# A graph kernel's projection with wo: the last 30 rows of wo in four groups of 32 array rows, results in the upper halves of four banks

## The reference, cut to what matters

```python
norm_x = t5_layer_norm(hidden_states, ln_weight)
y = jax.nn.elu(rgcn_conv(norm_x, edge_index, edge_type, W_rel, W_root, conv_bias))  # 1250 x 286
y = y @ wo_weight                                                                  # 286 x 1024
return hidden_states + y
...
x = _layernorm(x + _L0_gnn_ref(...), axis=-1)   # so x1 = layernorm(2x + elu(...) @ wo)
# second network: h = layernorm(x) * g + b; h = relu(h @ W1 + b1) @ W2 + b2; three graph layers; decoder
```

## Time and profile before

| | |
|---|---|
| median of 3 runs | 587.81 us (587.09 to 589.5) |
| profiled execution | 587.64 us |
| its span, first to last instruction | 585.8 us |
| mean granted TensorE clock | 0.992 |
| stage of the change (aggregation of ten tiles with projection) | about 167 to 273 us of the span |
| one steady tile of it | 10.3 us |

### The profile page before, as it was taken

The page is one execution under the profiler, slowest core; times in us unless marked ns, Lnnn a source line. Parts: engine busy times, 40 slices in busy tenths (PEclk is TensorE's granted clock), DMA queues, the critical chain, the costliest instruction groups (busy, mean ns, idle before and its releaser), DMA issues.

```text
span 585.8 us, 8370 instructions
## 1 busy us (share of the span) xinstructions
PE 570.0 (97%) x2584; PEld 395.6 (68%) x2584; DVE 379.7 (65%) x980; ACT 231.6 (40%) x477; POOL 100.7 (17%) x80
## 2 busy tenths in 40 slices
PE   7999999999999999999999999999999999999992
PEld 3556656665577676775898888877878867455541
DVE  7599888888847888888602330018748667755455
ACT  5444455533224546463421221013223134276555
POOL 3000000000000000003165512402202230132230
PEclk8999999999999999999999999999999999999997
DMA  9510011111031121128300000700100100021123
GB/s 270 145 35 10 27 36 35 35 35 35 0 92 37 35 72 37 38 76 237 129 27 0 0 0 1 223 4 1 38 0 0 36 1 0 2 70 49 58 70 105
DMA packets 20870, 30.73 MB, mean 52 GB/s; under 512 B 5428, under 2 KB 15254, under 8 KB 20838
## 3 DMA queue, kind: packets, MB, share of 16 engines
q1 hardware_dynamic: 20422, 29.66, 17.2%
q10 hardware_dynamic: 416, 0.67, 0.4%
HBM read 25.20 MB, written 5.12 MB: 52 GB/s over the span
## 4 chain that ended last, share of the span: by engine, by line
PE 94%; DMA 2%; DVE 2%; ACT 1%; POOL 0%; SPq 0%; issue 0%
PE banks L744 20%; PE banks L943 12%; PE banks L1029 12%; PE banks L863 12%; PE banks L730 5%; PE banks L833 5%; PE banks L965 4%; PE banks L955 4%; PE banks L892 4%; PE banks L894 4%; PE banks L873 3%; PE banks L1019 3%; PE banks L837 2%; PE banks L848 1%; PE banks L738 1%; DMA cb_b<-in_L_gnn_conv_bias 1%
## 5 line engine op out<-in xcount | busy, mean ns | idle before, releaser
L744 PE MATMUL banks<-w_all,xnT 128*125 128x429 f32 x320 | 130.4, 532 | 1.9 <-DMA w_all<-in_L_gnn_W_rel 1.9
L744 PEld LDWEIGHTS banks<-w_all,xnT 128*125 128x125 f32 x320 | 54.6, 190 | 32.1 <-issue 29.7
L1192 DVE TENSOR_TENSOR adj<-adj,banks 125x220 f32 x160 | 60.8, 380 | 19.5 <-PE banks L730 17.4
L863 PE MATMUL banks<-hT,w_s 128*128 128x250 f32 x320 | 68.7, 375 | 0.1
L863 PEld LDWEIGHTS banks<-hT,w_s 128*128 128x128 f32 x320 | 60.2, 189 | 8.8 <-issue 1.9
L892 PE MATMUL banks<-y_hi,adj 125*125 125x288 f32 x200 | 55.2, 304 | 0.2 <-issue 0.2
L894 PE MATMUL banks<-y_lo,adj 125*125 125x286 f32 x200 | 53.5, 294 | 0.0
L730 PEld LDWEIGHTS banks<-oh_code,oh_low 125*128 125x128 bf16 x320 | 31.0, 97 | 32.0 <-issue 27.9
L1174 DVE TENSOR_TENSOR oh_code<-iota_c,edge 125x880 bf16<-125x880 f16 x80 | 48.7, 609 | 0.0
L1336 DVE TENSOR_SCALAR hT<-banks,g_c,b_c 128x125 f32<-128x125 f32 x60 | 19.4, 400 | 45.1 <-PE banks L848 45.0
L943 PE MATMUL banks<-adj,h_hi 125*128 125x250 f32 (+1 forms) x180 | 48.2, 367 | 0.0
(11 more groups left out here) (206 smaller groups left out, 884.4 us busy)
## 6 DMA issues: line engine op xcount, KB each, us to landing
xt<-in_x SPq DMA_DIRECT2D x15, 448.0 KB
out_x<-ot SPq DMA_DIRECT2D x9, 448.0 KB
w_s<-in_L_gnn_W SPq DMA_DIRECT2D x5, 512.0 KB, 6.0
xn<-in_x SPq DMA_DIRECT2D x5, 448.0 KB
wd_s<-in_L_gnn_Wd SPq DMA_DIRECT2D x1, 2048.0 KB, 13.7
w_all<-in_L_gnn_W_rel SPq DMA_DIRECT2D x6, 286.0 KB, 6.8
wo_s<-in_L_gnn_wo_weight SPq DMA_DIRECT2D x1, 1024.0 KB, 6.5
w_all<-in_L_gnn_W_root SPq DMA_DIRECT2D x3, 286.0 KB, 6.4
```

The source lines that it names most:

```text
L744: ins = pe.matmul(pb[0:P, 2 + 2 * v + n, 0:FH], xnT[:, u], w_all[:, u, n * FH:(n + 1) * FH], start=(u == 0), stop=(u == KD - 1))
L863: ins = pe.matmul(pb[:, 4 + f % 2, 0:2 * P], w1_s[:, k, f * 128:(f + 1) * 128], hT[:, k], start=(k == 0), stop=(k == KD - 1))
L1192: dve.tensor_tensor(cols, cols, window(b, q), ALU.add).then_inc(done, 1)
```

## The change

It adds two constants, Q = 4 and QW = 256. The columns of wo are cut into four quarters. Each quarter has its own results bank, 4 + q, and there the upper half, columns 256 to 511. The last 30 rows are four logical matmuls on array rows 32q to 32q + 29. The transposes go to the lower halves of banks 4 and 5 (before: all in bank 4). Therefore `turn_elu(t)` gets a wait for `res_done`; the last tile's transposes go to banks 2 and 3 instead, and the second half of `turn_chunk(0)`, which writes those, gets a wait for `yT_copied`. Since bank 4 still holds results when the encoder begins, the first block of chunk 0 goes to bank 0, and chunk 0 is written out in front of the loop. `wo_mm` counts 4 per tile. SP loads the last rows of wo four times, a quarter each; VectorE writes the tails four times (120 elements of a 128-wide buffer) and reads the four half banks in the residual.

```diff
+Q, QW = 4, D // 4
...
-            ("ybuf", [P, 5, F], F32), ("yT", [128, 3, P], F32), ("tails", [P, 64], F32), ("mv", [P, T, 4], F32),
+            ("ybuf", [P, 5, F], F32), ("yT", [128, 3, P], F32), ("tails", [P, 32 * Q], F32), ("mv", [P, T, 4], F32),
...
-            for q in range(2):
-                sp.dma_start(wo_s[32 * q:32 * q + FB[2], 2, q * 512:(q + 1) * 512],
-                             wo[256:F, q * 512:(q + 1) * 512]).then_inc(wo_in, 16)
+            for q in range(Q):
+                sp.dma_start(wo_s[32 * q:32 * q + FB[2], 2, q * QW:(q + 1) * QW],
+                             wo[256:F, q * QW:(q + 1) * QW]).then_inc(wo_in, 16)
...
-            def turned(t):
+            def turned(t, b=4):
                 act.wait_ge(yT_ps, t + 1)
-                act.wait_ge(wo_mm, 1 + 2 * t)
-                act.copy(yT[:, 0:2].rearrange("p k n -> p (k n)"), pb[:, 4, 0:2 * P])
-                act.copy(yT[0:64, 2], pb[0:64, 4, 2 * P:3 * P]).then_inc(yT_copied, 1)
+                act.wait_ge(wo_mm, 1 + Q * t)
+                act.copy(yT[:, 0:2].rearrange("p k n -> p (k n)"), pb[:, b, 0:2 * P])
+                act.copy(yT[:, 2], pb[:, b + 1, 0:P]).then_inc(yT_copied, 1)
...
-            turned(T - 1)
+            turned(T - 1, 2)
...
-            def turn_elu(t):
+            def turn_elu(t, b=4):
 
                 pe.wait_ge(elu_done, t + 1)
+                if t > 0 and b == 4:
+                    pe.wait_ge(res_done, t)
                 for i in range(2):
-                    pe.transpose(pb[:, 4, i * P:(i + 1) * P], ybuf[:, 4, i * 128:(i + 1) * 128], ident[0:P, 0:P])
-                pe.transpose(pb[0:64, 4, 2 * P:3 * P], tails[:], ident[0:P, 0:P]).then_inc(yT_ps, 1)
+                    pe.transpose(pb[:, b, i * P:(i + 1) * P], ybuf[:, 4, i * 128:(i + 1) * 128], ident[0:P, 0:P])
+                pe.transpose(pb[:, b + 1, 0:P], tails[:], ident[0:P, 0:P]).then_inc(yT_ps, 1)
             def project(t):
...
-                for q in range(2):
+                for q in range(Q):
                     for i in range(2):
-                        pe.matmul(pb[0:P, 5 + q], yT[:, i], wo_s[:, i, q * 512:(q + 1) * 512],
+                        pe.matmul(pb[0:P, 4 + q, 512 - QW:512], yT[:, i], wo_s[:, i, q * QW:(q + 1) * QW],
                                   start=(i == 0), stop=False)
-                for q in range(2):
+                for q in range(Q):
                     rows = slice(32 * q, 32 * q + FB[2])
-                    ins = pe.matmul(pb[0:P, 5 + q], yT[rows, 2], wo_s[rows, 2, q * 512:(q + 1) * 512],
+                    ins = pe.matmul(pb[0:P, 4 + q, 512 - QW:512], yT[rows, 2], wo_s[rows, 2, q * QW:(q + 1) * QW],
                                     start=False, stop=True)
                     ins.then_inc(wo_mm, 1)
-            def turn_chunk(c):
+            def turn_chunk(c, shared=False):
                 for u in range(2):
+                    if shared and u == 1:
+                        pe.wait_ge(yT_copied, T)
...
-            turn_elu(T - 1)
-            turn_chunk(0)
+            turn_elu(T - 1, 2)
+            turn_chunk(0, True)
             project(T - 1)
 
-            with pe.Fori(0, T // 2 - 1) as c:
+            chunk_of_3(0, False, 0)
+            with pe.Fori(1, T // 2 - 1) as c:
                 chunk_of_3(c, False)
...
-                dve.scalar_tensor_tensor(tails[:].rearrange("p (q n) -> p q n", q=2)[:, :, 0:FB[2]], twice(exps), -1.0,
-                                         twice(above), ALU.add, ALU.add).then_inc(elu_done, 1)
+                dve.scalar_tensor_tensor(tails[:].rearrange("p (q n) -> p q n", q=Q)[:, :, 0:FB[2]], copies(exps), -1.0,
+                                         copies(above), ALU.add, ALU.add).then_inc(elu_done, 1)
...
-                dve.wait_ge(wo_mm, 1 + 2 * (t + 1))
+                dve.wait_ge(wo_mm, 1 + Q * (t + 1))
                 dve.wait_ge(x_in, 32 * (t + 1))
-                dve.scalar_tensor_tensor(x1(t), xt[:], 2.0, pb[0:P, 5:7].rearrange("p a b -> p (a b)"),
+                dve.scalar_tensor_tensor(x1(t).rearrange("p (q n) -> p q n", q=Q), xt[:].rearrange("p (q n) -> p q n", q=Q), 2.0, pb[0:P, 4:8, 512 - QW:512],
                                          ALU.mult, ALU.add).then_inc(res_done, 1)
```

More of the change, by code:

```diff
@@ L330, in _ @@
             sp.dma_start(wa_s[:], wa[0].rearrange("(k p) f -> p k f", p=128)).then_inc(wab_in, 16)
-            sp.wait_ge(wo_mm, 1 + 2 * T)
+            sp.wait_ge(wo_mm, 1 + Q * T)
             for a, d in ((bd2_b, bd2), (go_b, g_out), (bo_b, b_out)):
@@ L542, in weigh_first, with relus_of_3 @@
                 ins.then_inc(hT_lo, 1)
-            def relus_of_3(c, blocks):
+            def relus_of_3(c, blocks, b0=4):
                 for f in blocks:
@@ L548, in relus_of_3 @@
                     act.wait_ge(r1_mm, 1 + c * K1 + f + 1)
-                    act.activation(r1T[:, f], pb[:, 4 + f % 2, 0:2 * P],
+                    act.activation(r1T[:, f], pb[:, b0 if f == 0 else 4 + f % 2, 0:2 * P],
                                    ACT.Relu, bias=b1_c[:, f:f + 1]).then_inc(r1_done, 1)
@@ L568, in _ @@
             first_norm(T - 2)
-            relus_of_3(0, [0])
+            relus_of_3(0, [0], 0)
             first_sd(T - 1)
@@ L850, in turn_chunk, with chunk_of_3 @@
                         ins.then_inc(xhT_ps, 1)
-            def chunk_of_3(c, last):
+            def chunk_of_3(c, last, b0=4):
                 pe.wait_ge(hT_lo, 1 + c + 1)
@@ L862, in chunk_of_3 @@
                     for k in range(KD):
-                        ins = pe.matmul(pb[:, 4 + f % 2, 0:2 * P], w1_s[:, k, f * 128:(f + 1) * 128], hT[:, k],
+                        ins = pe.matmul(pb[:, b0 if f == 0 else 4 + f % 2, 0:2 * P], w1_s[:, k, f * 128:(f + 1) * 128], hT[:, k],
                                         start=(k == 0), stop=(k == KD - 1))
@@ L897, in relations @@
                     if t == 1:
-                        pe.wait_ge(wo_in, 48)
+                        pe.wait_ge(wo_in, 16 + 16 * Q)
                     if t > 0:
@@ L1258, in _, with copies @@
             sums, below, exps, above, elu = (ybuf[:, i] for i in range(5))
-            def twice(a):
-                return a[:, 256:F].rearrange("p (o n) -> p o n", o=1).broadcast_to([P, 2, FB[2]])
+            def copies(a):
+                return a[:, 256:F].rearrange("p (o n) -> p o n", o=1).broadcast_to([P, Q, FB[2]])
             def relations(t, b, adj):
```

## The result

The changed kernel took 585.36 us in the median of 8 runs (583.42 to 586.65), the kernel before 587.75 us in 8 runs beside it. The ratio is 0.9956, with a 95% interval of 0.9941 to 0.9972: 2.4 us faster between the medians, 0.44% by the ratio. In a second comparison it gave 0.9945 (0.9930 to 0.9960). The forecast was 584.2 us, in a range of 583.3 to 586.8. The profiled execution took 585.49 us with a span of 583.7.

A forecast was written before the change was run, and what follows sets the result against it. TensorE, busy for 97% of the span, was taken as the bound; nine tiles at 0.40 us give 3.6, less 0.11 for tile 0, 3.5 us off 587.64: 584.1, written as 584.2 us, range 583.3 to 586.8.

The forecast's parts named there:

- the line of a plain forecast: Whole time 584.9 us, about 0.5% (2.9 us) faster, distinguishable from no change; faster than that had chance 0.59.
- Four groups at once: Projection's last 30 rows: four row groups run together, block 0.63 us, 0.42 less; net 0.40 us less per tile.
- The rival of pairs: Projection's last 30 rows: only two row groups run at a time, block stays 1.05 us, whole time 587.9; chance 0.13.
- the one of groups in a row: Projection's last 30 rows: row groups run one by one, block 1.92 us, whole time 595.7; chance 0.04.
- A round costs more with four: Rival, projection's last 30 rows: each round 0.3 of a pass longer, 0.13 us per tile, whole time 585.4; chance 0.10.
- The added wait costs 0: Transposes waiting for the previous tile's residual: load 0.04 us late, up to 0.09 free, price 0 with 0.05 to spare.
- The rival of a pace set by VectorE: Residual or its signal reaches the transposes 0.25 us later: 1.4 us over seven tiles, whole time 585.6; chance 0.14.
- Eight tiles keep 0.40: Aggregation's loop, tiles 0 to 7, TensorE the bound: each keeps the 0.40 us gain, 8 x 0.40.
- Projection 8 is lost to xh: Before the encoder handover: TensorE comes 0.40 us earlier but waits 0.75 us for xh, not 0.35; nothing kept.
- Projection 9 keeps 0.40: Last projection, behind the xh wait: hT ready about 272.7, TensorE wants it at 273.03, so the 0.40 us is kept.
- Tile 0: First tile's tails on the chain: wider write 0.06 us, larger clear taken as 0.05, together +0.11 us once.
- wo's four small loads, ScalarE's copy, the new wait's cover: Side edits: SP's smaller transfers 0 (upper bound 0.8 us), 128-partition yT copy 0, last chunk turn's yT wait covered.

## Why the prediction was right, and where its sum was off

The direction and the range were right, and so was the mechanism of the gain; one term of the sum failed and two were mis-sized. Forecast gain 3.5 us, measured 2.4 (2.6 or 3.2 by the two comparisons' ratios); from the first transpose to the last matmul 397.13 and 397.18 us became 394.31 and 394.15, so 2.8 to 3.0, less 0.1 in tile 0. The 0.6 to 0.8 us that are missing there are in the terms below; the rest of the first comparison's distance is no larger than the scatter of the first stage. 585.36 us also lies on the far side of the 584.9 that was drawn as the line of a plain forecast, where the prediction had put its rivals (0.4% gain in the first comparison, 0.55% in the second).

- **Four groups at once**: right. Block 0.64 for 0.63, full-height part 3.46. Two groups alone give 1.06 and no gain. The rival of pairs and the one of groups in a row fall.
- **A round costs more with four**: falls too. Two rounds take 0.44 us with four groups for 0.43 of two passes, by the block of the kernel with two groups. The passes' records are 476 and 374 ns, apart by 0.10 as 689 and 587 were; nothing is added within a round. By an estimate from the Trainium skill's 3.07 times (TensorE: Matmul & The Clock Gate, Part 3) a round would have been 1.3 passes, 0.56 us for two; the trace doesn't agree, and what keeps the block of 0.64 us above half of before (1.05) is the 0.2 us for entering and leaving.
- **The added wait costs 0**: the step that failed. The sum had the residual seen 0.05 us after its end, a load 0.04 late, and 0.09 free. The end of the residual was forecast exactly (6.60). But the load starts 0.115 after it, because the late wait stands second behind another, so it is 0.10 late, of which some 0.07 are free. That leaves 0.03 to 0.04 in each of tiles 2 to 8, 0.18 and 0.26 in the loops of the two profiles. With one wait the forecast's reckoning comes true: 79.34 us. The rival of a pace set by VectorE had this path and put 0.25 us more on it, 1.4 us in all; it is right in kind, with less than a fifth of the price.
- **Eight tiles keep 0.40**: 82.48 - 79.34 = 3.14 without the wait's price, 2.96 and 2.88 with it; forecast 3.2 (8 x 0.40).
- **Projection 8 is lost to xh**: right (the load waits 0.6 us for xh, 0.75 was forecast, 0.35 before), and 0.12 more is lost, which the forecast set at nothing: it counted neither GpSimd beside the wider tails nor the second wait.
- **Projection 9 keeps 0.40**: mis-sized, 0.34 in the one profile and 0.08 in the other. I had checked hT and not what follows. Relu and norm of tile 9 on ScalarE, behind tile 9's x, came just in time for block 3 in the kernel before (the relu ended 0.18 us ahead of it), and TensorE's lead ran into them.
- **Tile 0**: clear and tails were set at 0.11; in the chain the clear's step is longer by 0.06 and the tails' by 0.06, 0.12 in all.
- **wo's four small loads, ScalarE's copy, the new wait's cover**: no wait names them; 0 each. The new wait for yT costs its 0.06 us only by standing in front of the late one.

## What to carry to other kernels

Short contractions that already run in two row groups can run in four: here the streaming time halved again, 0.86 to 0.43 us, and the fixed 0.2 us for entering and leaving stayed. Before a gain on the bounding engine is counted, look at each neighbour whose margin is smaller than that gain, and also at the stage after: here VectorE took back 0.03 us in each of seven tiles, GpSimd and a second wait 0.12 once, and a late x and ScalarE's order up to 0.3 once. In this kernel an added wait that came last cost less as the only one in front of its instruction; moving the work that it waits for forward in its engine's order did the same. Where runs scatter by more than the edit is worth, compare stages inside the traces, and look at the granted clock of each stage before a difference is put down to loads.

## What the runs showed of the hardware that was not expected

- A late wait that stands behind another one starts TensorE's load 0.115 us after the signalling instruction's end, a lone one 0.05 us after. It was so for VectorE's and for GpSimd's signal, and taking one wait away undid it in both places. Why, the trace doesn't show, and no run tries the two waits in the other order.
- A small VectorE instruction of 0.21 us in front of a large one delayed the large one's end by 0.08 us only.
- GpSimd's instruction grew by just as much (0.06 us) as VectorE's beside it, and shrank again with it.
- The same program ran its first products with w_all at 1.2 or at 2.4 GHz. In both profiles of the kernel before the first of them begins at 8.86 us; the seventh begins at 12.79 us where the granted clock had fallen to 0.50, and at 11.10 where it was 1.00. The aggregation then started at 167.57 and 166.61.
